# A residual added by GpSimd in one late group, and the first weights loaded pair by pair from two queues

## What is computed

```python
# x: (64, 64, 512) f32; conditions: 64 row numbers; weights: (200, 64, 64)
w = weights[conditions]                       # one 64x64 matrix for each of 64 samples
y = einsum('bct,bcd->bdt', x, w)              # "mix": 64x64 matrix times 64x512
a = quant_dequant_mxfp4(y)                    # blocks of 32 along t: shared power-of-two scale, e2m1 values
W = quant_dequant_mxfp4(ffn_weight)           # 512 x 512
out = x + einsum('mk,nk->mn', a, W) + bias    # residual, f32
```

## Time and profile before

| | us |
|---|---|
| median of 3 runs | 95.93 |
| lowest, highest | 95.76, 98.33 |
| the profiled execution, own time | 96.47 |
| its span, first to last instruction | 94.8 |
| VectorE busy | 83.3 (88%) |
| TensorE busy | 82.6 (87%) |
| ScalarE busy | 74.2 (78%) |
| GpSimd busy | 29.6 (31%) |
| mean granted TensorE clock | 0.973 of full |

### The profile page before, as it was taken

One profiled execution on the slowest core, in us unless ns is written; L12 is line 12 of the kernel. 1 busy time (PEld: TensorE's weight loads), 2 busy tenths in 40 slices (PEclk: granted clock), 3 DMA queues, 4 the chain that ended last, 5 costly groups with the idle time before them and its releaser, 6 DMA issues.

```text
span 94.8 us, 2110 instructions
## 1 busy us (share of the span) xinstructions
PE 82.6 (87%) x688; PEld 39.9 (42%) x695; DVE 83.3 (88%) x149; ACT 74.2 (78%) x86; POOL 29.6 (31%) x57
## 2 busy tenths in 40 slices
PE   4998499797989999999999999999989997999700
PEld 4954119186384234333523433352343334345400
DVE  1189984999999999999999999999999999999900
ACT  3736049999799759999999999999999977984100
POOL 4478885987788103000300300030030003030000
PEclk9999859999999999999999999999999999999996
DMA  1999699999999999999699999399289769829984
GB/s 23 297 306 267 149 378 280 364 343 291 328 321 287 336 294 249 198 302 239 144 202 302 322 275 181 124 274 228 47 286 239 138 246 250 168 92 271 317 297 137
DMA packets 14683, 23.20 MB, mean 245 GB/s; under 512 B 4178, under 2 KB 4946, under 8 KB 14674
## 3 DMA queue, kind: packets, MB, share of 16 engines
q1 hardware_dynamic: 11744, 17.83, 63.2%
q0 software_dynamic: 2256, 4.21, 21.1%
q10 hardware_dynamic: 674, 1.05, 3.8%
HBM read 11.54 MB, written 8.39 MB: 210 GB/s over the span
## 4 chain that ended last, share of the span: by engine, by line
DVE 64%; issue 5%; ACT 1%; DVEq 1%
DVE n_int L678 15%; DVE a L706 10%; DVE top L697 10%; DVE low L666 8%; DVE inv L671 4%; DVE amax L648 2%; DVE m L637 2%; DVE zone L684 2%; DVE last_x L812 2%; DVE m L631 2%; DVE m L643 1%; DVE x_sb L807 1%; DVE s L661 1%; DVE s L654 1%; ACT zone L520 1%
## 5 line engine op out<-in xcount | busy, mean ns | idle before, releaser
L378 PE MATMUL o_ps<-wT,aT 128*128 128x512 bf16 x98 | 23.5, 380 | 1.0 <-issue 1.0
L331 PE MATMUL y_ps<-x_sb,mix 64*64 64x512 f32 x128 | 18.3, 659 | 3.4 <-DMA mix<-in_L_cond_weights_dram 1.8
L504 ACT ACTIVATE z<-y_ps 128x1024 bf16<-128x1024 bf16 x16 | 16.3, 1035 | 5.4 <-PE y_ps L331 5.3
L678 DVE TENSOR_TENSOR n_int<-y_sb,inv 128x1024 int16<-128x1024 f32 (+1 forms) x18 | 19.6, 1100 | 0.3
L203 POOL DMA_DIRECT2D mix<-in_L_cond_weights_dram x32 | 16.9, 529 | 5.7 <-issue 4.5
L307 POOL DMA_DIRECT2D x_sb<-o_sb x6 | 5.3, 887 | 42.6 <-ACT o_sb L533 42.6
L406 PE MATMUL o_ps<-idle 128*128 128x128 bf16 x202 | 15.3, 233 | 1.2 <-DVE idle L711 1.2
L512 ACT COPY y_sb<-y_ps 128x1024 f32<-128x1024 f32 x16 | 16.3, 1039 | 0.0
L378 PEld LDWEIGHTS o_ps<-wT,aT 128*128 128x128 bf16 x104 | 9.0, 97 | 15.0 <-ACT aT L542 3.2
L406 PEld LDWEIGHTS o_ps<-idle 128*128 128x128 bf16 x202 | 12.7, 104 | 3.9 <-issue 3.6
L520 ACT ACTIVATE zone<-inv 128x1024 int16<-128x1024 int16 (+1 forms) x13 | 11.9, 938 | 0.3 <-DVE inv L671 0.2
(11 more groups left out here) (59 smaller groups left out, 76.2 us busy)
## 6 DMA issues: line engine op xcount, KB each, us to landing
x_sb<-in_x_dram SPq DMA_DIRECT2D x7, 1024.0 KB, 9.4
out_dram<-x_sb SPq DMA_DIRECT2D x16, 256.0 KB, 3.6
x_sb<-o_sb POOLq DMA_DIRECT2D x6, 512.0 KB, 5.6
out_dram<-x_sb SPq DMA_DIRECT2D x5, 512.0 KB, 2.8
w_sb<-in_L_ffn_weight_dram SPq DMA_DIRECT2D x4, 256.0 KB, 3.6
last_x<-in_x_dram SPq DMA_DIRECT2D x4, 256.0 KB, 7.7
x_sb<-in_x_dram SPq DMA_DIRECT2D x1, 512.0 KB, 6.5
mix<-in_L_cond_weights_dram SPq DMA_DIRECT2D x32, 16.0 KB, 7.1
```

Of the source, the lines that this page charges most:

```text
L331: last = nc.tensor.matmul(y_ps[HALVES[g], 2 * q + r, :], mix[HALVES[r], (step - 1) * GROUP + n, :], x_tiles(step, n)[HALVES[r], :], start= ...
L378: last = nc.tensor.matmul(o_bank(step, t), aT[:, t, c, :], wT[:, c, :], start=False, stop=(c == KC - 1))
L504: nc.scalar.activation(blocked(columns(z[:, step % 2, :, :], 2 * q, 2)), high_by_place(y_tiles(2 * q, 2)), ACT.Abs, scale=ZONE_GAIN).then_ ...
L678: nc.vector.tensor_tensor(columns(n_int, t, n), columns(y_sb[:, step % 2, :, :], t, n), columns(inv, t, n), ALU.mult).then_inc(n_done, 1)
```

## The change

Three edits.

1. Step 6 (the last but two), second pair. The accumulating DMA by POOL is gone for this step; instead GpSimd runs one `tensor_tensor` add of `o_sb` and x, 128 partitions by 1024 f32, into `x_sb`. POOL's own store (L311) is gone; SP waits for the add (`late_added`) and stores the pair with 512 KB, behind the two stores of step 6's first pair and ahead of those of step 7.
2. Step 1's matrices. POOL now loads those of tile 0, then those of tile 2; SP those of tile 1, then those of tile 3. Each pair has a semaphore of its own on each queue, and PE waits for each pair for two DMAs of POOL and two of SP (and x as before). From step 2 on all is as before.
3. `WARMUPS` goes from 20 to 21: four more idle matmuls before the first mix.

```diff
-WARMUPS = 20
+WARMUPS = 21
...
+            for q in range(2):
+                load_mixes(sp, mybir.EngineType.SP, sp_first_in[q], 1, range(2 * q + 1, 2 * q + 2))
+            load_mixes(sp, mybir.EngineType.SP, sp_mix_in[2], 2, SP_TILES)
...
+                elif step == LAST - 2:
+                    sp.wait_ge(late_added, 1)
+                    store(step, SUMMED, GROUP - SUMMED)
...
-            for step in range(1, 4):
-                load_mixes(pool, mybir.EngineType.Pool, pool_mix_in, step, POOL_TILES)
+            for q in range(2):
+                load_mixes(pool, mybir.EngineType.Pool, pool_first_in[q], 1, range(2 * q, 2 * q + 1))
+            for step in range(2, 4):
+                load_mixes(pool, mybir.EngineType.Pool, pool_mix_in[step], step, POOL_TILES)
...
-            for step in range(1, LAST - 1):
+            for step in range(1, LAST - 2):
 
                 pool.wait_ge(copied_out, 2 * step)
                 pool.dma_start(x_tiles(step, SUMMED, GROUP - SUMMED), o_sb[:, step % 2, :, :].rearrange("p t n -> p (t n)"),
                                accum_op=ALU.add).then_inc(x_added[step % 2], 16)
-            pool.wait_ge(x_added[(LAST - 2) % 2], 16 * ((LAST - 1) // 2))
-            n0 = (LAST - 3) * GROUP + SUMMED
-            pool.dma_start(out_dram[:, n0:n0 + 2, :], x_tiles(LAST - 2, SUMMED, 2).rearrange("p (n t) -> p n t", n=2)
-                           ).then_inc(late_stored, 16)
+            pool.wait_ge(copied_out, 2 * (LAST - 2))
+            late_x = x_tiles(LAST - 2, SUMMED, 2)
+            nc.gpsimd.tensor_tensor(late_x, o_sb[:, (LAST - 2) % 2, :, :].rearrange("p t n -> p (t n)"), late_x, ALU.add
+                                    ).then_inc(late_added, 1)
...
                 if step == 1:
                     pe.wait_ge(x_first_in[q], 16)
+                    pe.wait_ge(pool_first_in[q], 16 * MIXES // 4)
+                    pe.wait_ge(sp_first_in[q], 16 * MIXES // 4)
                 elif q == 0:
                     pe.wait_ge(x_in[step], 16)
-                if q == 0:
                     pe.wait_ge(pool_mix_in[step], 16 * MIXES // 2)
                 else:
                     pe.wait_ge(sp_mix_in[step], 16 * MIXES // 2)
```

More of the change, by code:

```diff
@@ L102, in adaln_ffn_program @@
         last_x_in = sem("last_x_in")
+        sp_first_in = [sem(f"sp_first_in_{q}") for q in range(2)]
+        pool_first_in = [sem(f"pool_first_in_{q}") for q in range(2)]
         sp_mix_in = [sem(f"sp_mix_in_{s}") for s in range(STEPS + 1)]
@@ L105, in adaln_ffn_program @@
         x_added = [sem("x_added_even"), sem("x_added_odd")]
-        stored, others_stored, late_stored = sem("stored"), sem("others_stored"), sem("late_stored")
+        stored, others_stored, late_added = sem("stored"), sem("others_stored"), sem("late_added")
         ident_clear, ident_ready = sem("ident_clear"), sem("ident_ready")
@@ L195, in load_first_x, with load_mixes @@
                             x_dram[:, 2 * q:2 * q + 2, :]).then_inc(x_first_in[q], 16)
-        def load_mixes(queue, engine, mix_in, step, tiles):
+        def load_mixes(queue, engine, done, step, tiles):
             first = (step - 1) * GROUP + tiles.start
@@ L203, in load_mixes @@
                 queue.dma_start(mix[HALVES[i % 2], first + i // 2, :],
-                                table[bass.ds(row, 1), :, :].rearrange("o c d -> (o c) d")).then_inc(mix_in[step], 16)
+                                table[bass.ds(row, 1), :, :].rearrange("o c d -> (o c) d")).then_inc(done, 16)
         def store_last(queue, t, g, part, done):
@@ L226, in _ @@
             sp.wait_ge(cond_in, 16)
-            load_mixes(sp, mybir.EngineType.SP, sp_mix_in, 1, SP_TILES)
-            load_mixes(sp, mybir.EngineType.SP, sp_mix_in, 2, SP_TILES)
+            for q in range(2):
+                load_mixes(sp, mybir.EngineType.SP, sp_first_in[q], 1, range(2 * q + 1, 2 * q + 2))
+            load_mixes(sp, mybir.EngineType.SP, sp_mix_in[2], 2, SP_TILES)
             load_x(2)
             load_x(3)
-            load_mixes(sp, mybir.EngineType.SP, sp_mix_in, 3, SP_TILES)
+            load_mixes(sp, mybir.EngineType.SP, sp_mix_in[3], 3, SP_TILES)
             load_x(4)
             for step in range(4, STEPS + 1):
-                load_mixes(sp, mybir.EngineType.SP, sp_mix_in, step, SP_TILES)
+                load_mixes(sp, mybir.EngineType.SP, sp_mix_in[step], step, SP_TILES)
                 if step + 1 <= STEPS:
@@ L263, in _ @@
                 store_last(sp, GROUP - 1, 0, n_half(half), stored)
-            sp.wait_ge(stored, 16 * (2 * (LAST - 1) + LAST - 3 + 2 + GROUP + 1))
+            sp.wait_ge(stored, 16 * (2 * (LAST - 1) + LAST - 2 + 2 + GROUP + 1))
             sp.wait_ge(others_stored, 16 * (GROUP + 1))
-            sp.wait_ge(late_stored, 16)
         @block.gpsimd
@@ L295, in _ @@
                                     ).then_inc(bias_step, 1)
-            load_mixes(pool, mybir.EngineType.Pool, pool_mix_in, 4, POOL_TILES)
+            load_mixes(pool, mybir.EngineType.Pool, pool_mix_in[4], 4, POOL_TILES)
             pool.wait_ge(bias_step, 4)
```

## The result

The changed kernel took 97.29 us in the median of 6 runs (97.08 to 99.11); the kernel before, run beside it, 96.28 (95.76 to 98.33). The interval lies above 1, but it includes 1.02, so whether the loss is more than 2% is not settled. The ratio leaves out executions more than 1.5% above the fastest of their kernel, and the one profiled ahead of the prediction is of that kind.

The account below looks back on a forecast made before the run. VectorE was taken to bound the kernel, with 64% of the chain. The sum 96.47 - 1.6 (start) + 2.0 (stop) - 0.6 (end) = 96.3 is 95.7 on the median's scale; range 93.5 to 97.0, the forecast's own 94.6 to 96.7.

Parts of the forecast that it names:

- the term of -1.6: Step 1's start: pair 0 at 10.0, clock stays full, VectorE's 1.55 us hole goes; gain 1.6 us, range 1.1 to 1.7.
- 0.54: Amount by which the median of the runs lies below the profiled execution of 96.47 us; turns 96.3 into 95.7.
- The stop: At step 6's GpSimd add: VectorE's `rescale` waits until 80.45, a loss of 2.0 us; bounds nothing, 1.4, 2.7.
- the forecast 2.2 us: Length of the GpSimd add of 1024 f32, taken as the middle of 1.5 and 2.8 us.
- The relief at the end: Last stores: issuing step 6's 512 KB earlier takes it out of the crowded stretch; gain 0.6 us, ends 0 and 1.0.
- its own figure of 93.8: Last burst: ten stores issued from 88.3, moving from about 90.3, need 3.5 us at 300 GB/s and end at 93.8.
- B: Rival: pair 0 stays near 10.8, the start gives only 0.2, the add still stops VectorE; 97.1 us, chance 0.14.

Follow-up runs that it names:

- before_again: The kernel before with no edit, run once more for a second profile; its four executions took 94.97, 96.43, 97.42 and 97.47 us.
- warm21_only: The kernel before with 21 warm-up rounds in place of 20 and the old order of loads; 95.85 us, ratio to before 1.0063.
- tail_only: The kernel before with the GpSimd add and SP's store alone, the start as before; 97.56 us, ratio to before 1.0239.
- head_only: The kernel before with the pair-by-pair loads and 21 warm-up rounds alone, the old end kept; 95.35 us, ratio to before 1.0028.
- after_look_4: The changed kernel with no edit, run again in search of a profile without the lower clock near 80 us; 97.41 us.
- pe_busy: The changed kernel with 24 idle matmuls on TensorE ahead of the second transposes of step 7; 96.05 us, ratio to before 1.0133.
- no_add: The changed kernel without the GpSimd add, SP storing after ScalarE's copy, that pair's residual sum left out; 94.76 us, ratio to before 0.9899.

## Why the prediction was wrong

The forecast failed first at the term of -1.6: "the 16 matmuls of two pairs took 3.37 us here", the clock falls, and the change takes that away. The trace was read rightly, and the changed kernel did what was said (pair 0 at 9.63 for 10.0, 1.09 us for a pair, no hole, 1.5 us for 1.6). But the hole of 1.55 us belongs to a part of the executions only: `before_again` has it (2.52), `warm21_only` has 0.57 of it, and `tail_only`, at a full clock with pair 0 at 10.59, has none. The sum then took off 0.54 as well, to come from the profiled execution to the median. As far as the profiles show, executions of the usual time have less of the hole or none, so the same time was in part counted twice. The signs that the execution was not typical were there: its own time lay 0.54 above the median, the fastest run was at 95.76, and two pairs of 1.0 us from 10.8 with the second `z` (1.02) behind them end at 13.8, just when VectorE is free (13.83). In the comparison the term of -1.6 is 0 (`head_only`, 1.0028).

Measured against the profiled execution itself, the start did hold, and the miss is at the end. The forecast for it was 96.47 - 1.6 + 2.0 - 0.6 = 96.3; the changed kernel's profile has 97.33. Start and stop account for 0.1 us of the difference each. The other 0.8 lies behind `rescale`: -0.6 was forecast for that stretch, and +0.2 came, as 1.13 later at the last add less 0.9 behind it, and in `after_look_4` as nothing at the last add and 4.9 behind it for 4.7.

The stop was right: 2.0 forecast, 2.13 measured, through both steps (GpSimd served when `limit` ends, 2.2 us from then). Only the instruction that is held up is another: `lowest_zone`, one earlier than `rescale`; a `tensor_scalar` waits as well. That the add took the forecast 2.2 us is in part luck: it was the middle of 1.5 and 2.8, worked out from two selects of different types.

So a second step failed, a term that was missing: TensorE idle behind VectorE's stop and its clock, +1.13 between `rescale` and the last add in the profile. It was not asked what waits for the stopped engine. `after_look_4` and the four executions at a full clock say that in the changed kernel it hardly counts at the end, because without it the transfers take as much longer; `pe_busy` says that it can be won, and why there alone is open.

The relief at the end was forecast with 0.6; `no_add` against `head_only` gives 0.6, and the two profiles of before and after 0.9, but `after_look_4` against before gives -0.2. The mechanism, less data in the last burst, was right as far as it goes; that this burst alone, and not the last add, can set the end was not drawn from its own figure of 93.8. Nor do the ranges fit together: the ends given for the terms add up to 95.93 - 1.1 + 2.7 = 97.5, the text says 97.1, and the range given for the forecast stops at 96.7.

With the first term at 0 the sum is 2.1 + 0 to 1.1 - 0.6 to 0.9, between 1.2 and 2.6; measured were 1.9 (1.0195 of about 95.4) and for `tail_only` 2.3. Of the rivals B was nearest, at 97.1 and with 0.14: its mechanism (the second loads land late) was wrong, since pair 0 did start early, but its result, a start that gives nothing, was right.

## What to carry to other kernels

Before a wait in one profile is counted as something to win, hold the profiled execution's time against the other runs and ask whether the wait would be there at the clock that most of them have. An elementwise add moved to GpSimd is not off VectorE's path: in this kernel VectorE stood still for all of its 2.1 us, whole or in pieces. When one engine is to be stopped, look who waits for it, and at the end of a kernel check whether transfers in flight would have covered the gain or the loss.

## What the runs showed that was not expected

- The four pieces of the add stretch four VectorE instructions of two kinds by 0.52 to 0.54 us each, so the two engines go in turn, one instruction each.
- The new load order took nothing off the median and yet narrowed the spread from 93.98 to 98.02 (67 executions) to 94.86 to 96.00 (16).
- The changed kernel's last burst of stores has two forms: 4.9 us behind the last add with a gap in the transfers (0.47 busy for 2 us) and one DMA issue of 1.22 us in place of 0.35 ahead of it, or 3.5 to 3.9 us without.
- A mean clock of 0.982 stood for a fall near 80 us in one execution and for a fall behind the last add, which costs nothing, in another.
